# One change to a four-layer transformer kernel: the second attention's scores issued by number, a third stack buffer, updates behind the stacks, function tables loaded ahead

## The chip, the cores and the metric

The kernel runs on one core of a Trainium2 chip. A core has TensorE (PE, matrix products; its weight loads are listed as PEld), VectorE (DVE), ScalarE (ACT), GpSimd (POOL) and SyncE (SP, which issues DMAs). Each engine works through its own queue in order, and the queues meet only through semaphores. The metric is the device time of one execution in microseconds (us), lower is better.

## The reference

Tokens are 2 sequences (b) of 512 positions with 256 features, in 8 tiles of 128 tokens. Four layers run one after the other, each of the same form:

```python
for l in range(4):
    xn = layernorm(x)
    s = attn[l](xn)
    g = silu(ffn[l](xn))
    x = x + s * g
```

Layer 0: causal attention of 16 heads of 16, then a mixture of 8 experts with a shared one, sigmoid gated. Layer 1, the one the change is about, has 16 query heads, 4 key heads and no mask:

```python
q, k = rms_norm(xn @ Wq), rms_norm(xn @ Wk); v = xn @ Wv
q, k = rope(q), rope(k)
probs = softmax(einsum('btkgh,bskh->bkgts', q * H**-0.5, k))
out = einsum('bkgts,bskh->btkgh', probs, v) @ Wo
```

Its FFN sends every token to 2 of 8 experts. Layers 2 and 3 are causal attentions of 16 heads of 128 with plain FFNs of 1024 hidden features (GELU), the last one with ternary weights and a 4-bit rounding of its output.

## The kernel before

All work is written out by hand, one block per engine; the order within an engine is the order of the calls in its block, and nothing reorders it. Waits count: `x.wait_ge(sem, n)`.

**Stacks.** Scores of layers 0 and 1 are kept exact with bf16 matrices: every query and key of 16 numbers is split into three bf16 parts and stacked into 96 rows. In layer 1 a tile m (8 of them, 4 per sequence) takes this path: PE projects it (`project1`, line 761), ACT takes it out of the bank with its squares (`take`), POOL and DVE rotate it, ACT writes the first parts (`stack1_first`, lines 1412 to 1414), DVE the remainders (`stack1_rest`, 1901), POOL the middle parts (`stack1_middle`, 520), DVE the last ones (`stack1_last`, 1911), PE transposes the stack (`stack1_transpose`, 728: 20 matrices into three banks), and ACT and DVE copy it out (`stack1_copy`, 1366, and `stack1_copies`, 1920 to 1924). Tiles 0 to 3 do so while layer 0's FFN ends (`ffn0`), tiles 4 to 7 inside the loop of the second attention. The last four have two buffers (`STK1B`), so tile 6 waits for tile 4's transposes and tile 7 for tile 5's.

**Second attention.** `attention1` has 32 steps s, four to a unit u (a sequence and a group of 4 heads). In step s ACT takes 4 exponentials (line 1482) of 128x512 scores out of banks 0, 1, 2 in turn into one of two halves of PT. PE computes scores n = 4s to 4s+3 (line 882), each into bank n % 3, so score n waits for exponential n-3. `values(s)` (line 893) multiplies the 4 probabilities of step s with V into bank 4 and waits for all four. The order on PE is

```python
scores(0)
for s in range(UNITS1 * TPB):
    if s + 1 < UNITS1 * TPB: scores(s + 1)
    if s % TPB == 0 and s > 0: turn_outputs(s // TPB - 1)
    values(s)
    ...   # s 3: layer norm transposes; 4, 5, 6: project1; 10-13: stack transposes; 15: ranks
```

At a unit's end DVE stores bank 4 (`store_outputs`, 1984), PE turns it (`turn_outputs`, 901) and DVE divides (`normalise`, 1974 and 1975); the first `values` of a unit waits for the store of the unit before. ACT has its own extra work behind the exponentials of a step: two copies after step 4, `take` after 5 (two), 6 and 7, `router_act` after 8, `stack1_first` after 9 to 12. DVE works through rotations, the router's small operations (`probabilities`, `largest`, `chosen`, `slots`, some 0.25 us each) and stacks in an order written out.

**End of the first FFN.** `ffn0` computes 13 hidden chunks per sequence: PE (line 1159) into one of three pairs of banks, ACT a sigmoid (1629), POOL or DVE (600, 2169) the weighting, DVE the product (`hidden`, 2170 and 2174), and PE's chunk after the next two waits for that product. Four tiles of output follow per sequence: `down` on PE (1177), `tail` on DVE (2159), `post` on ACT (1635), `update` on DVE (2153 to 2155, into X). `post` and `update` have two pairs of buffers. For the second sequence they are mixed with the stacks of tiles 0 to 3.

**Function tables.** ACT holds one set of functions. Where the next activation needs another, the program has an ACT_TABLE_LOAD right ahead of it; copies need none.

## Time and profile before

| | us |
|---|---|
| median of 3 runs (lowest, highest) | 1364.73 (1360.65, 1364.87) |
| the profiled execution's own time | 1354.29 |
| span of its trace | 1352.5 |
| PE busy | 1223.2 (90%) |
| DVE, ACT, POOL busy | 731.8, 604.8, 122.9 |
| mean granted TensorE clock, share of full | 0.984 |

The profile's page has the busy time of each engine, the span in 40 slices, and the chain that ended last: from the last instruction back, at each step to what released it. The timeline lists instructions in order of time: start in us from the span's start, duration, engine, line, operation, written tile <- read tile with their shapes, how many equal ones were merged, and in brackets how long the engine stood idle before them and who released it. The view by windows gives busy time per engine (with the number of instructions), the granted clock as a share of 2.4 GHz, the share of DMA time, and GB/s. Instructions overlap in their pipelines: four exponentials of 0.6 us start 0.49 us apart.

### The profile page before, as it was taken

What the parts mean: (1) busy time and instruction counts of PE and PEld (TensorE: products, weight loads), DVE (VectorE), ACT (ScalarE), POOL (GpSimd) and SP (SyncE); (2) the same over time, 40 slices, a digit from 0 to 9 for tenths busy, and PEclk for the clock granted to TensorE, in tenths of its full rate; (3) what the DMA queues carried; (4) which work ended last, traced back from release to release, by engine and by line L of the source; (5) the groups of instructions that cost most, each with busy time, mean ns of one, the idle gap of its engine ahead of it and who ended that gap; (6) DMA issues with size and microseconds to landing.
All of it is one profiled execution on the core that took longest, in us unless ns stands there. A gap on an engine that the chain in (4) does not pass through costs nothing.

```text
span 1352.5 us, 18754 instructions
## 1 busy us (share of the span) xinstructions
PE 1223.2 (90%) x6390; PEld 763.2 (56%) x6396; DVE 731.8 (54%) x2031; ACT 604.8 (45%) x1511; POOL 122.9 (9%) x144
## 2 busy tenths in 40 slices
PE   5988878878899979999999899999999999999994
PEld 4634444423276545656565587656666666667853
DVE  3776627826143478787878720444444444447257
ACT  2634543677822224545455402444454454442053
POOL 3320013421400400000000000000000000000000
PEclk9989999999999989999999999999999999999998
DMA  8001000320222400000000002100000000000000
GB/s 245 1 18 41 33 27 0 103 72 1 94 78 90 187 12 12 12 12 13 8 8 8 1 0 74 67 24 12 24 12 24 13 24 16 20 12 1 1 0 31
DMA packets 28046, 48.66 MB, mean 36 GB/s; under 512 B 3902, under 2 KB 22302, under 8 KB 26886
## 3 DMA queue, kind: packets, MB, share of 16 engines
q1 hardware_dynamic: 25222, 38.13, 8.8%
q0 software_dynamic: 2736, 9.37, 2.4%
q8 instruction: 53, 0.87, 0.3%
q14 instruction: 35, 0.29, 0.1%
HBM read 40.36 MB, written 9.19 MB: 37 GB/s over the span
## 4 chain that ended last, share of the span: by engine, by line
PE 67%; DVE 13%; issue 11%; ACT 6%; POOL 2%; DMA 1%; SPq 0%; ACTq 0%; POOLq 0%; DVEq 0%
PE bank L975 13%; PE bank L991 9%; PE bank L982 8%; PE bank L968 5%; PE bank L960 5%; PE bank L986 4%; PE bank L893 2%; PE bank L1221 2%; PE bank L882 2%; PE bank L1312 2%; PE bank L1239 2%; PE bank L1159 2%; PE bank L814 1%; ACT PT L1482 1%; PE bank L1299 1%
## 5 line engine op out<-in xcount | busy, mean ns | idle before, releaser
L1366 ACT COPY R<-bank 128x512 f32<-128x512 f32 (+4 forms) x199 | 106.3, 551 | 319.9 <-PE bank L991 142.8
L2052 DVE CUSTOM_DVE_ANT_0 bank<-bank,mask_row 128x128 f32<-128x128 f32 (+3 forms) x256 | 127.1, 497 | 173.2 <-PE bank L982 170.8
L975 PE MATMUL bank<-XNT,W 128*128 128x512 f32 x416 | 200.2, 605 | 7.4 <-ACT R L1366 3.8
L1511 ACT ACTIVATE R<-bank,nm 128x128 f32<-128x128 f32 (+3 forms) x256 | 136.2, 532 | 109.0 <-DVE nm L2052 108.1
L982 PE MATMUL bank<-R 128*128 128x512 f32 (+3 forms) x384 | 134.3, 434 | 0.0
L975 PEld LDWEIGHTS bank<-XNT,W 128*128 128x128 f32 x416 | 75.1, 191 | 100.9 <-issue 92.3
L960 PE MATMUL bank<-W,R 128*128 128x256 f32 x576 | 125.3, 380 | 3.2 <-ACT R L1366 3.2
L960 PEld LDWEIGHTS bank<-W,R 128*128 128x128 f32 x576 | 109.1, 190 | 18.7 <-ACT R L1366 2.1
L986 PE MATMUL bank<-identf,R 128*128 128x128 f32 x640 | 112.4, 275 | 7.1 <-DVE R L2069 5.5
L991 PE MATMUL bank<-PT,R 128*128 128x128 f32 (+3 forms) x384 | 112.0, 435 | 5.6 <-ACT PT L1366 4.3
L1366 ACT COPY PT<-bank 128x128 f32<-128x128 f32 (+3 forms) x256 | 108.6, 426 | 15.2 <-PE bank L986 15.1
L986 PEld LDWEIGHTS bank<-identf,R 128*128 128x128 f32 x640 | 79.2, 141 | 59.1 <-issue 33.7
L991 PEld LDWEIGHTS bank<-PT,R 128*128 128x128 f32 x384 | 71.2, 190 | 61.4 <-issue 37.8
L968 PEld LDWEIGHTS bank<-W,XNT 128*128 128x128 f32 x640 | 76.5, 192 | 9.5 <-issue 7.6
L968 PE MATMUL bank<-W,XNT 128*128 128x128 f32 x640 | 77.9, 275 | 0.0
L1482 ACT ACTIVATE PT<-bank 128x512 f32<-128x512 f32 x128 | 66.0, 607 | 15.1 <-PE bank L882 15.1
L1956 DVE TENSOR_REDUCE W<-bank 128x1 f32<-128x128 f32 (+3 forms) x128 | 55.9, 485 | 25.2 <-PE bank L778 24.9
L1471 ACT ACTIVATE PT<-bank 128x512 f32<-128x512 f32 (+3 forms) x128 | 46.2, 438 | 37.9 <-PE bank L804 37.5
L982 PEld LDWEIGHTS bank<-R 128*128 128x128 f32 x384 | 58.2, 191 | 1.1 <-issue 0.5
L882 PE MATMUL bank<-R 96*128 96x512 bf16 x128 | 40.9, 404 | 18.8 <-ACT PT L1482 17.8
L2069 DVE TENSOR_SCALAR R<-R,erec 128x128 f32<-128x128 f32 (+3 forms) x128 | 50.4, 394 | 5.2
L2115 DVE TENSOR_SCALAR R<-R,erec 128x128 f32<-128x128 f32 (+3 forms) x128 | 49.5, 387 | 5.1
(282 smaller groups left out, 1811.9 us busy)
## 6 DMA issues: line engine op xcount, KB each, us to landing
W<-in_wq SPq DMA_DIRECT2D x32, 128.0 KB, 2.0
W<-in_wo SPq DMA_DIRECT2D x2, 2048.0 KB, 11.4
W<-in_egu SPq DMA_DIRECT2D x1, 2816.0 KB
W<-in_wk SPq DMA_DIRECT2D x20, 128.0 KB, 2.1
W<-in_wv SPq DMA_DIRECT2D x20, 128.0 KB, 2.0
R<-xg SPq DMA_DIRECT2D x5, 512.0 KB, 4.7
yg<-R SPq DMA_DIRECT2D x5, 512.0 KB, 3.1
W<-in_wa SPq DMA_DIRECT2D x2, 1024.0 KB, 5.0
```

The source lines that it names most:

```text
L882: ins = mm(PS[n % 3][:, :], kstk[0:KQ, g, b * SEQ + j * P:b * SEQ + (j + 1) * P], qstk[0:KQ, g * GH + h, b * SEQ:(b + 1) * SEQ], start=Tru ...
L960: ins = mm(PS[4 + m % 4][:, 0:D], heads[:, k, m * P:(m + 1) * P], w[:, k, :], start=k == 0, stop=k == n - 1)
L968: ins = mm(bank[:, t * P:(t + 1) * P], XNT[:, c, b * SEQ + t * P:b * SEQ + (t + 1) * P], wqkv23[:, 2, c, :], start=c == 0, stop=c == DC - 1)
L975: ins = mm(bank[:, :], wqkv23[:, s, c, :], XNT[:, c, b * SEQ:(b + 1) * SEQ], start=c == 0, stop=c == DC - 1)
L982: return mm(PS[u % 4][:, 0:n], q[:, t * P:n], k[:, 0:n], start=True, stop=True)
L986: ins = tr(PS[4 + u % 2][:, j * P:(j + 1) * P], Pr[u % 4][:, j * P:(j + 1) * P], identf[:, :])
L991: ins = mm(PS[6][:, j * P:SEQ], v[:, j, :], PT[:, slot, j, j * P:SEQ], start=j == 0, stop=j == TPB - 1)
L1366: return nc.scalar.copy(dst, src)
L1482: fn(PT[:, s % 2, h, :], PS[n % 3][:, :], ACT.Exp, scale=HD ** -0.5).then_inc(cb["pb_ready"], 1)
L1511: return fn(Pr[c][:, 0:n], PS[c][:, 0:n], ACT.Exp, scale=-1.0, bias=nm[:, c:c + 1], accum_out=esum[:, c:c + 1])
L1956: dve.tensor_reduce(nmx[b][:, t, h:h + 1], PS[banks[i % len(banks)]][:, 0:(t + 1) * P], AX.X, ALU.max, negate=True).then_inc(smax_used, 1)
L2052: return dve.tensor_tensor_reduce(out=s[:, 0:n], in0=s[:, 0:n], in1=mask_row[:, SEQ - n:SEQ], scale=-1.0, scalar=-MASKED, op0=ALU.add, op1 ...
```

## The change

Seven edits, none of which changes a number that is computed:

1. `scores` in `attention1` counts single matrices instead of steps. Step s issues scores up to 4s+6, then `values(s)`, then scores up to 4s+9, and only then `turn_outputs` and the step's extra work. The waits of every score are as before.
2. Extra work is regrouped: `project1(7)` with `project1(6)` in step 5, both `take` after step 6, `stack1_first` one step earlier (8 to 11), `router_act` behind the second of them.
3. `STK1B` has three buffers, so that only tile 7 waits for a transpose (tile 4's). `RES1B` moves to R1.
4. On DVE, `probabilities(1)` and `largest(0)` go between and behind the first stacks of the loop.
5. `update` of tile 3 goes behind `hidden(1, 3)`, the updates of tiles 4 to 7 behind the last stack's copies. For that, tiles 4 to 7 have buffers of their own.
6. ACT's order at the end of `ffn0` is new.
7. A one-column activation `preload(func)` makes ACT load a table early: Sigmoid after the first attention, Exp ahead of the last stack's copy, Silu after the second attention, Exp after two FFNs, Gelu after attentions 2 and 3, Silu after the last hidden chunk.

```diff
-        STK1B = [R2[:, 2048 + 960 * i:3008 + 960 * i].bitcast(BF16).rearrange("p (h k e) -> p h k e", k=BLK, e=HD)
-                 for i in range(2)]
+        STK1B = [R2[:, 1024 + 960 * i:1984 + 960 * i].bitcast(BF16).rearrange("p (h k e) -> p h k e", k=BLK, e=HD)
+                 for i in range(3)]
...
-            return (STK1[m % 3], RES1[m % 2]) if m < TPB else (STK1B[m % 2], RES1B[m % 2])
+            return (STK1[m % 3], RES1[m % 2]) if m < TPB else (STK1B[m % 3], RES1B[m % 2])
...
+                issued = [0]
+
+                def scores(upto):
+                    for n in range(issued[0], min(upto + 1, UNITS1 * TPB * GH)):
+                        s, h = n // GH, n % GH
...
+                        if n % (NG * TPB * GH) == 0:
+                            pe.wait_ge(stk_act, 2 * NT + TPB)
+                            pe.wait_ge(stk_dve, 2 * NT + STACKS_A + STACKS_B * b)
                         pe.wait_ge(cb["pb_ready"], n + 1 + GH - 3)
...
+                    issued[0] = max(issued[0], upto + 1)
...
-                scores(0)
                 for s in range(UNITS1 * TPB):
-                    if s + 1 < UNITS1 * TPB:
-                        scores(s + 1)
+                    scores(s * GH + 6)
+                    values(s)
+                    scores(s * GH + 9)
                     if s % TPB == 0 and s > 0:
                         turn_outputs(s // TPB - 1)
-                    values(s)
...
                         project1(6)
-                    elif s == 6:
                         project1(7)
...
+            def preload(func):
+                fn(small[:, 62:63], mhalf[:, 0:1], func)
...
-                elif m >= TPB + 2:
-                    act.wait_ge(stk_ps, 4 * NT + 3 * (m - 1))
+                elif m == TPB + 3:
+                    act.wait_ge(stk_ps, 4 * NT + 3 * (TPB + 1))
...
                         take(6)
-                    elif s == 7:
                         take(7)
-                    elif s == 8:
-                        router_act(1)
-                    elif s in (9, 10, 11, 12):
-                        stack1_first(s - 5)
+                    elif s in (8, 9, 10, 11):
+                        stack1_first(s - 4)
+                        if s == 9:
+                            router_act(1)
...
                 stack1_first(1)
-                post(4)
-                post(5)
                 stack1_first(2)
                 stack1_copy(0)
-                post(6)
+                post(4)
                 stack1_first(3)
                 stack1_copy(1)
+                post(5)
+                post(6)
+                stack1_copy(2)
                 post(7)
-                stack1_copy(2)
+                preload(ACT.Exp)
                 stack1_copy(3)
...
                     if t >= 1:
                         update(t - 1)
-                    if t == TPB - 1:
-                        update(t)
                     hidden(1, t)
+                update(TPB - 1)
...
                 stack1_copies(3)
-                update(7)
+                for tile in range(TPB, NT):
+                    update(tile)
```

The other `preload` calls and the regrouped lines on DVE are as the list says.

PE in the second attention from the values of step 27 to those of step 29 before (line 882 scores, 893 values, 901 the turn of a unit's outputs):

```order
L893 MATMUL bank4<-PT,R2 32x512 x4
L882 MATMUL bank2<-R1 128x512
L882 MATMUL bank0<-R1 128x512
L882 MATMUL bank1<-R1 128x512
L882 MATMUL bank2<-R1 128x512
L901 MATMUL bank6<-identf,R2 128x128 x4
L893 MATMUL bank4<-PT,R2 32x512 x4
L882 MATMUL bank0<-R1 128x512
L882 MATMUL bank1<-R1 128x512
L882 MATMUL bank2<-R1 128x512
L882 MATMUL bank0<-R1 128x512
L893 MATMUL bank4<-PT,R2 32x512 x4
```

and of the changed kernel, the same stretch (886 scores, 897 values, 905 the turn):

```order
L897 MATMUL bank4<-PT,R2 32x512 x4
L886 MATMUL bank1<-R1 128x512
L886 MATMUL bank2<-R1 128x512
L886 MATMUL bank0<-R1 128x512
L886 MATMUL bank1<-R1 128x512
L897 MATMUL bank4<-PT,R2 32x512 x4
L886 MATMUL bank2<-R1 128x512
L886 MATMUL bank0<-R1 128x512
L886 MATMUL bank1<-R1 128x512
L905 MATMUL bank6<-identf,R2 128x128 x4
L886 MATMUL bank2<-R1 128x512
L897 MATMUL bank4<-PT,R2 32x512 x4
```

The third score of a step's successors stays ahead of the values, the fourth and two more come behind them, and the turn stands behind those instead of ahead of the values.

ACT at the end of `ffn0` before (1412 to 1414 `stack1_first`, 1366 a stack's copy, 1635 `post`, 1482 the first exponentials):

```order
L1366 COPY R1<-bank0 96x8x128
L1635 ACTIVATE R2<-R2 128x256
L1412 ACTIVATE PT<-R1,small 128x16x48
L1413 ACTIVATE PT<-R1,small 128x8x16
L1414 ACTIVATE PT<-R1,small 128x4x16
L1366 COPY R1<-bank3 96x8x128
L1635 ACTIVATE R2<-R2 128x256
L1366 COPY R1<-bank0 96x8x128
L1366 COPY R1<-bank3 96x8x128
L1482 ACT_TABLE_LOAD
L1482 ACTIVATE PT<-bank0 128x512
```

and of the changed kernel (1417 to 1419, 1368, 1639; 1371 is `preload`; the first exponential is the next row):

```order
L1368 COPY R1<-bank0 96x8x128
L1639 ACTIVATE R2<-R2 128x256
L1417 ACTIVATE PT<-R1,small 128x16x48
L1418 ACTIVATE PT<-R1,small 128x8x16
L1419 ACTIVATE PT<-R1,small 128x4x16
L1368 COPY R1<-bank3 96x8x128
L1639 ACTIVATE R2<-R2 128x256 x2
L1368 COPY R1<-bank0 96x8x128
L1639 ACTIVATE R2<-R2 128x256
L1371 ACT_TABLE_LOAD
L1371 ACTIVATE small<-mhalf 128x1
L1368 COPY R1<-bank3 96x8x128
```

Both `post` calls of tiles 5 and 6 are behind the last `stack1_first`, and the table load has moved from ahead of the exponentials to ahead of the last stack's copy.

DVE at the end of the first sequence's outputs before (2159 `tail`, 2153 to 2155 `update`, 2170 `hidden`, 1766 statistics):

```order
L2159 TENSOR_TENSOR R2<-bank7,XN 128x256
L2153 TENSOR_TENSOR R2<-R2 128x256
L2154 TENSOR_TENSOR R2<-R2 128x256
L2155 TENSOR_TENSOR X<-X,R2 128x256
L2153 TENSOR_TENSOR R2<-R2 128x256
L2154 TENSOR_TENSOR R2<-R2 128x256
L2155 TENSOR_TENSOR X<-X,R2 128x256
L2170 TENSOR_TENSOR W1<-R1,bank4 128x512
L1766 BN_STATS stat<-X 128x6 x4
```

and of the changed kernel (2171, 2165 to 2167, 2182, 1778):

```order
L2171 TENSOR_TENSOR R2<-bank7,XN 128x256
L2165 TENSOR_TENSOR R2<-R2 128x256
L2166 TENSOR_TENSOR R2<-R2 128x256
L2167 TENSOR_TENSOR X<-X,R2 128x256
L2182 TENSOR_TENSOR W1<-R1,bank4 128x512
L2165 TENSOR_TENSOR R2<-R2 128x256
L2166 TENSOR_TENSOR R2<-R2 128x256
L2167 TENSOR_TENSOR X<-X,R2 128x256
L1778 BN_STATS stat<-X 128x6 x4
```

The second `update` (tile 3) now stands behind the product that PE waits for.

## Rows read from the trace of the kernel before

**Rows 1.** The page's chain that ended last, shares of the span by engine.

```profile
PE 67%; DVE 13%; issue 11%; ACT 6%; POOL 2%; DMA 1%; SPq 0%; ACTq 0%; POOLq 0%; DVEq 0%
```

**Rows 2.** Timeline, a plain step and a turn step: start, us, engine, line, op.

```profile
340.03 2.06 ACT L1482 ACTIVATE PT<-bank 128x512 f32<-128x512 f32 x4 [0.39 <-PE bank L882]
340.68 0.39 PE L882 MATMUL bank<-R 96*128 96x512 bf16 x1 [0.32 <-ACT PT L1482]
341.00 1.07 PE L893 MATMUL bank<-PT,R 128*32 128x512 f32 x8
342.00 0.82 PE L882 MATMUL bank<-R 96*128 96x512 bf16 x3
342.49 2.06 ACT L1482 ACTIVATE PT<-bank 128x512 f32<-128x512 f32 x4 [0.39 <-PE bank L882]
...
343.36 0.60 PE L901 MATMUL bank<-identf,R 128*128 128x128 f32 x4
...
345.38 0.60 ACT L1482 ACTIVATE PT<-bank 128x512 f32<-128x512 f32 x1 [0.83 <-PE bank L882]
```

**Rows 3.** Timeline of ACT, attention's first exponentials, two waits, last exponentials.

```profile
268.09 4.03 ACT L1482 ACTIVATE PT<-bank 128x512 f32<-128x512 f32 x8
...
301.74 0.26 ACT L1378 ACTIVATE rt<-rt 128x64 f32<-128x64 f32 x1 [2.08 <-DVE rt L1800]
...
317.40 0.94 ACT L1412 ACTIVATE R<-R,small 128x768 bf16<-128x768 f32 x1 [1.35 <-PE bank L728]
...
368.37 2.07 ACT L1482 ACTIVATE PT<-bank 128x512 f32<-128x512 f32 x4 [0.39 <-PE bank L882]
```

**Rows 4.** Timeline of PE: last stack's transposes, first scores, one projection.

```profile
263.91 1.29 PE L728 MATMUL bank<-identb,PT 128*96 128x128 bf16 x20 [3.11 <-DVE PT L1913]
266.13 1.44 PE L882 MATMUL bank<-R 96*128 96x512 bf16 x3 [0.93 <-ACT R L1366]
...
290.34 1.59 PE L761 MATMUL bank<-W,XNT 128*128 128x393 f32 x4
```

**Rows 5.** Timeline of DVE: the last stack's remainders.

```profile
260.74 0.48 DVE L1901 SCALAR_TENSOR_TENSOR PT<-R,small,PT 128x256 f32<-128x256 f32 x1 [0.45 <-ACT PT L1414]
```

**Rows 6.** Timeline of ACT: the function table ahead of the first exponential.

```profile
266.80 1.28 ACT L1482 ACT_TABLE_LOAD   x1 [1.23 <-PE bank L882]
```

**Rows 7.** Timeline of all engines, first FFN: its start and its half's end.

```profile
191.05 2.54 PE L1159 MATMUL bank<-R,W 128*128 128x512 bf16 x11
191.43 1.28 ACT L1629 ACT_TABLE_LOAD   x1
...
226.09 2.54 POOL L600 TENSOR_TENSOR R<-R,W 128x512 f32<-128x512 f32 x2 [4.98 <-ACT R L1629]
...
226.24 1.38 DVE L2153 TENSOR_TENSOR R<-R 128x256 f32<-128x256 f32 x1
...
230.02 3.67 PE L1159 MATMUL bank<-XNT,W 128*88 128x512 f32 x8 [3.56 <-DVE W L2170]
...
233.50 1.38 DVE L1776 TENSOR_SCALAR XN<-X,mv,rstd 128x256 f32<-128x256 f32 x4
```

**Rows 8.** Timeline, start of the fourth layer's FFN.

```profile
1288.14 2.54 PE L1325 MATMUL bank<-R,W 128*128 x11 [0.42 <-ACTq L1716]
1288.14 1.28 ACT L1721 ACT_TABLE_LOAD   x1
```

**Rows 9.** Timeline of DVE: eighth stack's copies, then output store of unit 3.

```profile
325.95 0.69 DVE L1920 COPY R<-bank 96x1024 bf16<-96x1024 bf16 x1 [1.52 <-PE bank L728]
...
331.52 0.69 DVE L1984 COPY R<-bank 128x512 f32<-128x512 f32 x1 [0.34 <-PE bank L893]
```

**Rows 10.** Timeline of SP: the first loads of sorted rows for the experts.

```profile
362.01 15.70 SPq L424 DMA_DIRECT2D R<-xg  x3
```

**Rows 11.** Windows: PE, PEld, DVE, ACT, POOL busy us; granted clock; DMA share; GB/s.

```profile
266.00:273.00 7.00, 5.69 (x17) 1.05 (x18) 4.38 (x16) 5.31 (x9) 1.27 (x2) 0.52 0.99 269
...
329.30:370.50 41.20, 36.04 (x225) 9.54 (x223) 10.15 (x36) 33.09 (x65) 16.58 (x19) 1.00 0.22 77
```

55 lines of the change are left out of this document (27 added, 28 removed).

## The prediction, made before the changed kernel ran

> **What bounds the kernel now.** I read the page's chain first: two thirds of the span are matrix work of PE [rows 1], most of it in layers 2 and 3, which the change leaves alone but for some table loads. What it touches lies between 191 and 371 us, so there I read the timeline, and in it who ended each wait.
>
> In the second attention, the steps from 16 on show the rhythm [rows 2]. Call the end of a step's last exponential E. PE issues a score 0.05 after the exponential that frees its bank (340.03 + 0.60 is 340.63; the score starts at 340.68), `values` 0.32 later, the next score 1.00 after that (342.00), its exponential 0.49 later, and 0.61 later that has ended: 0.05 + 0.32 + 1.00 + 0.49 + 0.60 = 2.46 us, and the steps are 2.46 apart. ACT alone would need 4 x 0.49 = 1.96. So it is a ring of both engines, with each idle for part of it. A step with `turn_outputs` takes 345.38 - 342.49 = 2.89: the turn stands inside the ring and adds 0.43. All 32 steps take 370.44 - 268.09 = 102.35 us [rows 3]. Of these 4.03 are the first two steps [rows 3] and 30 x 2.46 = 73.8 the rhythm of the rest; 24.5 us are excess, from turns and from the extra work of steps 3 to 15.
>
> Ahead of it, PE stands 3.11 us for the last stack of tile 3, then 0.93 for ACT's last copy [rows 4], and ACT loads the Exp table for 1.28 when the first scores are already there [rows 6].
>
> **Part one: start of the first FFN.** The Sigmoid load ends at 192.71. PE's first chunk is four of the eleven matmuls that take 2.54 from 191.05 [rows 7], so ready at about 192.1. The load moves ahead of ACT's copies, where ACT waits for PE. Gain 0.6 at most, and the ring of chunk, sigmoid, weighting and product carries it on; if DVE's or POOL's start is bound otherwise, 0. I take 0.5.
>
> **Part two: `update(3)` behind `hidden(1, 3)`.** Before, DVE does the update from 226.24 while POOL works on two weightings in a row (2.54 for both), its first operation lasts 1.38, and PE stands 3.56 until 230.02 [rows 7]. The product needs POOL's first weighting, 226.09 + 1.27 = 227.4, plus 0.7 on DVE: PE can go on at 228.1, 1.9 sooner. But the update now falls under POOL's second weighting, statistics and normalisation still start when they did, and the layer norm's transposes wait for the scaling, 233.50 to 234.9 [rows 7]. PE's next two chunks wait for products that DVE has no sooner. What is left of the 1.9 at those transposes is 0.8. Bounds 0.2 and 1.9; I take 0.8.
>
> **Part three: the stacks of tiles 0 to 3.** Tile 2's transposes end at 263.91 - 3.11 = 260.80. Tile 3's wait because DVE has updates and `tail` between its pieces and its remainder waits 0.45 for ACT [rows 5], which did `post` calls first. In the new order ACT's first parts of tile 3 come at about 254.8, DVE's remainder at 258.2 (behind the copies of tile 1), POOL's parts by 260.0, DVE's last part by 260.5: tile 3's transposes follow tile 2's without a wait and end at 262.1. DVE's copies end near 263.0. ACT: copy of tile 2 until 261.0, `post(7)` 0.35, table load 1.28 [rows 6], the one-column activation 0.2, copy of tile 3 with 1.0: 263.8. So the load now holds up the last copy. Scores follow as before, 0.55 behind the copy, at 264.35, and the first exponential about 0.6 later at 264.9, against 268.09 [rows 3]: 3.2 us. Lower bound 1.3 (only the load leaves the scores), upper bound 3.11 + 1.28 = 4.4. The four updates, some 1.4 each, now run beside the first exponentials until 268.5; with statistics (1.8), POOL's 1.4 and the scaling (1.4) the second half's normalised tiles are ready at 273. The transposes that read them come at about 277, so this is covered by 4 us; without cover it would cost what is missing one for one.
>
> Here the Trainium skill speaks against the change: "ScalarE: Activation LUTs", section "What ACT_TABLE_LOAD costs", puts a switch at 1283 ns of load and about 1380 ns of drain, 2.66 us in total. The load here is 1.28, and the activation starts as it ends, at 268.09 with no second gap [rows 3, 6]. By the page the last copy would be held 1.38 longer than I have it and the sum would be 9.3 instead of 10.7.
>
> **Part four: scores by number.** Put the ring together again. Score 4s+6 needs exponential 4s+3, `values(s)` needs the same one, then come 4s+7 to 4s+9. From E: 0.05 + 0.32 + 1.00 + 0.49 + 0.60, again 2.46. The order doesn't shorten a plain step; it only cuts the ring at another exponential. But PE has issued score 4s+9 at E + 2.0 and needs to be back only at E + 2.5, so a turn (0.43) fits there. Seven turns gain 7 x 0.43 = 3.0, and `ranks` (0.4) goes the same way, as far as the store of unit 3 lets it.
>
> For steps 3 to 15 I followed both queues with the durations of the rows: exponentials 0.49 apart, a score 0.21, `values` 1.0, a projection 1.43 [rows 4], its `take` 0.98, `stack1_first` 1.37 [rows 3], a stack's transposes 1.25 (1.29 with the last one's drain) [rows 4], DVE's copies of a stack 1.54 [rows 9]. Counted from the first exponential, step 1 ends at 5.48 (later than before, since `values(0)` now stands ahead of its last score) and then 30 steps of 2.46 give 79.3. To this come as excess: step 5 0.8 (layer norm copies), 6 3.8 and 7 3.3 (four projections and their takes, little better than before), 9 to 11 2.8 (`stack1_first`, with the exponentials stalled behind it), 12 2.1 (tile 7's buffer waits for tile 4's transposes), 13 and 14 1.9, 15 2.0 (tile 7's transposes wait 1.4 for DVE's copies of tile 6), 17 0.4 (the store of unit 3 is behind `largest` and `chosen`; before, these and the copies filled DVE from 325.95 to 331.52 [rows 9]). That is 17.2 in place of 24.5, and the whole 96.5 against 102.35: 5.8 us, turns included. Gone are the 2.08 that ACT waits for the router [rows 3], since first stack work now stands ahead of it, and part of the waits of 1.35 for a stack's transposes [rows 3]. Lower bound 3.0, the turns alone; upper bound 10, if DVE's waits vanish too.
>
> **The clock.** From 266 to 273 the granted clock is 0.52 of full, that is the 1.2 GHz level, after PE had stood for 3.11 and 0.93 us; from 329.3 to 370.5 it is 1.00 [rows 4, 11]. But it had stood 3.56 us before 230.02 [rows 7], and the matmuls behind that ran at full speed (3.67 for 8). With one wait of 2.3 instead of two, full speed at the first scores would gain 0.9 more (`values(0)` 1.7 against 1.0, and a score); I take 0.4 between 0 and 0.9.
>
> **Part five: the other loads.** Each is worth 1.28 at most. The one ahead of the last FFN starts at 1288.14 together with PE's matmuls, of which the first chunk is six of eleven in 2.54, so 1.4: it was hidden [rows 8]. The others stand where ACT waits for PE anyway. The eight one-column activations are 0.2 each, one of them counted above. I take 0 for all; bounds -0.5 and 1.3.
>
> **What comes behind.** The experts need rows that POOL scatters; the first load is issued at 362.01 [rows 10], 8.4 us before the last exponential ends, and it depends on `normalise(5)`, which moves with the loop. It stays covered by some 4 us.
>
> **Sum.** 0.5 + 0.8 + 3.2 + 5.8 + 0.4 = 10.7 us. The profiled execution took 1354.29, so 1343.6 in its terms; its span of 1352.5 becomes 1341.8. The median of the runs is 10.4 higher; I carry the difference over to it: 1364.73 - 10.7 = 1354.0.
>
> **The rivals.** *The load hurts more where it stands now*: the last stack's copy is held by more than the 1.28, say by as much again, and 1.4 are lost: 1355.4. Against it: no gap behind a load [rows 3, 6]. 0.09. The drain in "ScalarE: Activation LUTs" of the Trainium skill (section "What ACT_TABLE_LOAD costs") would do just this; so far the trace does not bear it out. *A new wait takes the old one's place*: DVE's queue, with its many small operations, is late with a store or a copy in steps 10 to 17, and in the stack part only the load's 1.3 is won: 0.5 + 0.8 + 1.3 + 3.0 = 5.6, 1359.1. For it: my working of 13 steps has a dozen meeting points, and any error there costs. 0.18. *The scores' order does nothing*: a plain step keeps 2.46 in any case, and if the turn's bank isn't stored in time, it falls back into the ring; then 2.6 is left, 1362.1, no measurable change. Against it: the store starts right behind `values` and takes 0.7, while the turn stands 1.6 behind the next step's start. 0.12. *Slower*: the clock. The new order spreads PE's waits differently, and if PE is granted 1.2 GHz in the loop, a plain step grows by about 0.7 for `values`, 0.2 for the third score and 0.2 for the next: 1.1. It takes back the gain after 10 steps and is slower by over 0.3% from the 14th; 31 steps give 1364.7 - 10.7 + 34 = 1388. Against it: 1.00 in the same loop before, with as much waiting [rows 2, 11]. 0.05.
>
> **How the numbers follow.** A measurement of this kernel can tell 0.3%, about 4 us. My forecast of 1354.0 has 0.56. Faster: 0.56 + 0.09 + 0.18 = 0.83; within 0.3%: 0.12; slower: 0.05. The parts' bounds around the forecast and the new wait's 1359 give 1347 to 1361; the runs' own spread of 4 us is inside that.
>
> **What would show it.** Step distances of 2.46 at the turns (wrong: 2.9). The first exponential about 4.5 sooner (0.5 + 0.8 + 3.2), near 263.6. The table load directly ahead of the last stack's copy, and no wait for tile 3's transposes. The last exponential near 360.2. PE back at about 228 in the first FFN, but only 0.8 ahead at the layer norm's transposes. It would be wrong if PE stands for DVE in steps 10 to 17 longer than 2 us in all, or if the granted clock falls below 1.00 in the loop.

## The result, and the profile after

| | before | after |
|---|---|---|
| median of 4 runs (lowest, highest), us | 1362.86 (1360.65, 1364.87) | 1348.22 (1345.48, 1350.60) |
| ratio, 95% interval | | 0.9896 (0.9878 to 0.9915) |
| the profiled execution's own time, us | 1354.29 | 1347.06 |
| span of its trace, us | 1352.5 | 1345.3 |
| mean granted clock | 0.984 | 0.984 |

The change gains 14.2 us by the ratio, where 10.7 were forecast; the two traces differ by only 7.2. Both gaps need an account, and most of the experiments went into it. In the table above, before has four runs. The forecast was counted down from the 1364.73 of three of them, so 1.9 us of the distance between 1354.0 and 1348.22 lies in that starting point.

The page of after has its first lines and its chain as follows; the chain is as in [rows 1], since what the change touches is a tenth of the span.

```profile
span 1345.3 us, 18762 instructions
PE 1225.4 (91%) x6396; PEld 765.1 (57%) x6396; DVE 731.3 (54%) x2031; ACT 605.4 (45%) x1518; POOL 121.5 (9%) x144
PE 69%; DVE 13%; issue 10%; ACT 7%; POOL 1%; DMA 0%; SPq 0%; ACTq 0%; POOLq 0%; DVEq 0%
```

**Start of the first FFN** (timeline of after, PE and ACT). The Sigmoid load is gone from ahead of the first sigmoid, which starts 1.06 behind PE's chunk. PE's two chunks with a wait start 11.22 us (185.40 to 196.62) behind the out projection, against 12.05 (183.83 to 195.88) before: 0.8 gained. The out projection itself started 1.57 later than in the first trace of before, where nothing is changed.

```profile
192.41 2.75 PE L1161 MATMUL bank<-R,W 128*128 128x512 bf16 x12
193.47 0.60 ACT L1633 ACTIVATE R<-bank 128x512 f32<-128x512 f32 x1 [0.49 <-PE bank L1161]
196.62 3.03 PE L1161 MATMUL bank<-R,W 128*128 128x512 bf16 x12 [1.46 <-DVE R L2182]
```

**Update of tile 3 behind the product** (timeline of after, the rows that answer to [rows 7]). PE's wait is 1.65 instead of 3.56. But the normalisation (DVE L1788) now lasts 2.22 instead of 1.38, beside POOL's weighting of 234.61, and the second pair of transposes waits for it. The first project starts at 237.78.

```profile
228.84 3.67 PE L1161 MATMUL bank<-XNT,W 128*88 128x512 f32 x8 [1.65 <-DVE W L2182]
234.04 2.22 DVE L1788 TENSOR_SCALAR XN<-X,mv,rstd 128x256 f32<-128x256 f32 x4
234.61 1.18 POOL L602 TENSOR_TENSOR R<-R,W 128x512 f32<-128x512 f32 x1 [0.93 <-ACT R L1633]
236.31 0.66 PE L683 MATMUL bank<-identf,XN 128*128 128x128 f32 x4 [0.66 <-DVE XN L1788]
237.78 5.68 PE L763 MATMUL bank<-W,XNT 128*128 128x393 f32 x16
```

**Stacks of tiles 0 to 3** (timeline of after, answering to [rows 3, 4, 6]). The transposes of tiles 2 and 3 are one row of 40. The load stands ahead of the last copy and holds it up, the scores follow 0.06 behind the copy, and the granted clock is 1.00 from the first score on, where it was 0.52 [rows 11].

```profile
259.85 2.52 PE L730 MATMUL bank<-identb,PT 128*96 128x128 bf16 x40
261.40 0.42 ACT L1639 ACTIVATE R<-R 128x256 f32<-128x256 f32 x1
261.84 1.28 ACT L1371 ACT_TABLE_LOAD   x1
263.24 0.99 ACT L1368 COPY R<-bank 96x1024 bf16<-96x1024 bf16 x1
264.29 0.82 PE L886 MATMUL bank<-R 96*128 96x512 bf16 x3 [1.91 <-ACT R L1368]
264.77 3.54 ACT L1487 ACTIVATE PT<-bank 128x512 f32<-128x512 f32 x7 [0.54 <-PE bank L886]
```

**The loop** (timeline of after). Answering to [rows 2]: plain steps are 2.40 apart, not 2.46 (332.00, 334.40), and a step with a turn is 2.41 (357.51 to 359.92, the turn at 357.75) instead of 2.89. The loop takes 362.92 - 264.77 = 98.15 against 102.35. Three of its steps are 3.95, 3.52 and 3.65 long, though nothing but scores, values and one turn is in them: 3.9 us together. The rows show two kinds of time in them. In the first and the third, ScalarE stands although its scores are ready. The second is TensorE at half clock behind the first: `values` takes 1.94 instead of 1.06, and the granted clock is 0.54 from 339 to 342. In the kernel without early loads (below) the clock stays at 1.00 behind the same first pause, and the step is 2.42. "Pauses" below means the sum of both kinds.

```profile
332.00 2.06 ACT L1487 ACTIVATE PT<-bank 128x512 f32<-128x512 f32 x4 [0.33 <-PE bank L886]
334.40 2.06 ACT L1487 ACTIVATE PT<-bank 128x512 f32<-128x512 f32 x4 [0.33 <-PE bank L886]
338.35 2.06 ACT L1487 ACTIVATE PT<-bank 128x512 f32<-128x512 f32 x4 [1.89 <-PE bank L886]
341.87 2.06 ACT L1487 ACTIVATE PT<-bank 128x512 f32<-128x512 f32 x4 [1.45 <-issue]
345.52 2.06 ACT L1487 ACTIVATE PT<-bank 128x512 f32<-128x512 f32 x4 [1.58 <-PE bank L886]
357.75 0.60 PE L905 MATMUL bank<-identf,R 128*128 128x128 f32 x4
362.32 0.60 ACT L1487 ACTIVATE PT<-bank 128x512 f32<-128x512 f32 x1 [0.33 <-PE bank L886]
```

PE in the second of these steps, the window of after (columns: stretch, its length, busy time and instructions of PE, PEld, DVE, ACT, POOL, then the granted clock, DMA share, GB/s), and the like window of the kernel without early loads:

```profile
339.36 1.94 PE L897 MATMUL bank<-PT,R 128*32 128x512 f32 x8
339.00:342.00 3.00, 2.99 (x11) 0.58 (x12) 0.00 (x0) 1.55 (x4) 2.13 (x3) 0.54 0.24 87
```

```profile
341.00:344.00 3.00, 2.74 (x17) 0.62 (x20) 0.00 (x0) 2.67 (x6) 2.09 (x4) 1.00 0.24 87
```

### The profile page after: what moved, and what is told of

Its sections match the earlier page's. It is cut to its first block, busy times and chain, and to the rows that moved or that the text cites. A ratio compares the mean times of both kernels' runs of the same rounds, so it can differ in the third digit from the quotient of the medians.

```text
span 1345.3 us, 18762 instructions
## 1 busy us (share of the span) xinstructions
PE 1225.4 (91%) x6396; PEld 765.1 (57%) x6396; DVE 731.3 (54%) x2031; ACT 605.4 (45%) x1518; POOL 121.5 (9%) x144
## 4 chain that ended last, share of the span: by engine, by line
PE 69%; DVE 13%; issue 10%; ACT 7%; POOL 1%; DMA 0%; SPq 0%; ACTq 0%; POOLq 0%; DVEq 0%
PE bank L977 13%; PE bank L993 9%; PE bank L984 8%; PE bank L962 5%; PE bank L970 5%; PE bank L988 4%; PE bank L1223 2%; PE bank L886 2%; PE bank L897 2%; ACT PT L1487 2%; PE bank L1314 2%; PE bank L1274 2%; PE bank L1241 2%; PE bank L816 1%; PE bank L1301 1%
## 5 line engine op out<-in xcount | busy, mean ns | idle before, releaser
L1968 DVE TENSOR_REDUCE W<-bank 128x1 f32<-128x128 f32 (+3 forms) x128 | 56.1, 484 | 26.1 <-PE bank L780 25.8
```

The lines of the kernel that those rows point to most:

```text
L1968: dve.tensor_reduce(nmx[b][:, t, h:h + 1], PS[banks[i % len(banks)]][:, 0:(t + 1) * P], AX.X, ALU.max, negate=True).then_inc(smax_used, 1)
```

## The experiments

**How they are read.** One trace is one draw, so each is cut into stretches that can be set side by side: from the first `down` of the first FFN to the first exponential, the loop, and the units of the loop, counted between DVE's stores (`store_outputs`). A unit without other work is 10.27 us in the old order of scores, 9.60 in the new one, 10.03 with the turn in the ring and some 11.96 with the values in halves; what stands above that in units six and seven is called pauses. All lengths are in us. The changed kernel was also run a second time without an edit ("after, again"). It was expected, before that run, to have pauses of 2.5 to 4.5 us at the same steps if they are the usual case, and a first unit of 10.8 at full clock if the early Exp load is what keeps the clock. Both came: 3.9 and 10.8.

| kernel | ratio to before (95%) | `down` to 1st exp. | loop | first unit | units 2 to 4 | units 6, 7 | pauses |
|---|---|---|---|---|---|---|---|
| before, first trace | | 56.1 | 102.35 | 12.4 | 19.2, 16.4, 15.4 | 10.3, 10.3 | 0 |
| before, again | 0.999 (0.9973 to 1.0007) | 57.6 | 106.5 | 12.3 | 19.2, 16.4, 15.4 | 14.5, 10.3 | 4.2 |
| scores alone | 0.9929 (0.9907 to 0.9950) | 57.0 | 102.7 | 12.7 | 17.3, 13.4, 19.0 | 13.1, 10.0 | 3.9 |
| regrouping alone | 0.9969 (0.9938 to 1.0000) | 57.0 | 105.3 | 13.1 | 18.4, 15.4, 13.2 | 15.6, 11.2 | 6.3 |
| FFN end alone | 0.9957 (0.9941 to 0.9972) | 52.4 | 107.4 | 12.9 | 19.2, 15.7, 15.7 | 15.2, 10.3 | 5.0 |
| after | 0.9896 (0.9878 to 0.9915) | 52.1 | 98.15 | 10.8 | 17.6, 16.2, 13.3 | 12.4, 10.7 | 3.9 |
| after, again | 0.9909 (0.9882 to 0.9937) | 52.1 | 98.2 | 10.8 | 17.6, 16.2, 13.3 | 12.5, 10.7 | 3.9 |
| no early loads | 0.9902 (0.9877 to 0.9927) | 52.4 | 98.6 | 12.4 | 17.6, 16.2, 13.3 | 12.4, 9.5 | 2.7 |
| no early Exp | 0.9914 (0.9894 to 0.9933) | 52.4 | 98.6 | 11.9 | 17.6, 16.2, 13.3 | 12.4, 10.0 | 3.2 |
| update 3 as before | 0.9899 (0.9880 to 0.9919) | 53.9 | 98.2 | 10.8 | 17.6, 16.2, 13.3 | 12.5, 10.7 | 4.0 |
| turn in the ring | 0.9920 (0.9901 to 0.9940) | 52.1 | 101.7 | 10.8 | 17.1, 16.2, 12.3 | 16.4, 10.7 | 7.1 |
| late scatters | 0.9988 (0.9970 to 1.0005) | 52.1 | 106.2 | 11.9 | 17.6, 16.2, 13.3 | 9.6, 9.6 | 11.7, in unit 8 |
| tanh | 0.9876 (0.9847 to 0.9905) | 51.1 | 96.95 | 10.8 | 17.6, 16.2, 13.3 | 12.4, 9.5 | 2.7 |
| values in halves | 0.9968 (0.9954 to 0.9983) | 52.1 | 108.5 | 14.2 | 18.4, 16.2, 14.1 | 12.0, 12.0 | 0 |

### The kernel before, once more

No edit.

> The kernel before, unchanged, once more: it sizes what differs between two executions of one program, since the profiled one of before took 1354.29 us and its timed ones 1360.65 to 1364.87. Theory A, the traced execution was a short draw: ratio 1.000 (within 0.2%), and a second trace has a span some 4 to 10 us above 1352.5, with the surplus in stretches that the change doesn't touch (start of the input loads, layer 0, layers 2 and 3), while the second attention keeps 102.35 us. Theory B, a profiled execution of before is always some 8 us short of its timed ones: span again near 1352. Theory C, the surplus lies in the second attention or the first FFN: then what the change gains is more than the first trace shows.

A span of 1365.5, 13.0 above the first trace. It lies in four places: 1.9 ahead of the first `down`, 1.5 from there to the layer norm's transposes, 4.1 in the loop, 4.5 between the experts and the shared expert, the rest 1.0. Theory A holds for the ratio and for the draw, but not for the place: 5.6 of the 13.0 lie where the change works, so theory C is right there. The first trace of before, on which the prediction was built, happened to have neither the half clock in the first FFN nor the pauses in the loop. The timeline of this trace, PE and ACT, at both places:

```profile
231.86 5.17 PE L1159 MATMUL bank<-XNT,W 128*88 128x512 f32 x8 [3.56 <-DVE W L2170]
...
343.25 2.07 ACT L1482 ACTIVATE PT<-bank 128x512 f32<-128x512 f32 x4 [0.39 <-PE bank L893]
345.71 2.06 ACT L1482 ACTIVATE PT<-bank 128x512 f32<-128x512 f32 x4 [0.39 <-PE bank L893]
350.58 2.06 ACT L1482 ACTIVATE PT<-bank 128x512 f32<-128x512 f32 x4 [2.80 <-remote]
351.77 1.94 PE L893 MATMUL bank<-PT,R 128*32 128x512 f32 x8
354.86 1.08 ACT L1482 ACTIVATE PT<-bank 128x512 f32<-128x512 f32 x2 [2.21 <-PE bank L893]
...
365.57 2.06 ACT L1482 ACTIVATE PT<-bank 128x512 f32<-128x512 f32 x4 [0.39 <-PE bank L893]
```

The same wait of 3.56 as in [rows 7] is followed here by 5.17 us for the 8 matmuls that took 3.67. In the loop the step from 345.71 to 350.58 is 4.87; behind the first pause `values` takes 1.94 instead of 1.06, so it costs clock as well. The last row names `values` (L893) as what an exponential waited for; it is used below.

### Scores by number alone

```diff
-                        scores(s + 1)
+                    scores(s * GH + 6)
+                    values(s)
+                    scores(s * GH + 9)
```

> The kernel before with edit 1 alone (scores by number, values ahead of the last three, turn behind them). The prediction's own terms: turns 3.0, ranks 0.4, a plain step unchanged at 2.46, so the loop takes about 99.0 instead of 102.35 and the ratio is 0.9975. Rival 1, the plain step is shortened too (the trace of after has steps of 2.40): 28 x 0.06 = 1.7 more, loop 97.3, ratio 0.996. If the steps are 2.46 here, the 2.40 belongs to something else. Rival 2, the order does nothing: the turn falls back into the ring, turn steps of 2.89, loop 102, ratio 1.000.

Plain steps are 2.40 apart here too, and turns stand outside them. The loop without its 3.9 of pauses is 98.8, 3.5 less than 102.35: nearer the first forecast (99.0) than rival 1 (97.3), though the shorter step is real, so rival 1 has the mechanism and not the size. The shares differ: units two and three lose 5.0, unit four gains 3.6 (the stacks' extra work now falls into it), and the plain units lose 0.67 each. The time fell by more than that (9.7 by the ratio, 6.8 at the least); this trace is the slowest of its six timed runs, so the loop's 3.5 is what is shown for the edit, and the rest is not accounted for.

### Regrouping alone

```diff
-            return (STK1[m % 3], RES1[m % 2]) if m < TPB else (STK1B[m % 2], RES1B[m % 2])
+            return (STK1[m % 3], RES1[m % 2]) if m < TPB else (STK1B[m % 3], RES1B[m % 2])
```

with the regrouped `project1`, `take`, `stack1_first`, and DVE's order.

> The kernel before with edits 2 to 4 alone (extra work regrouped, third stack buffer, DVE's small operations behind the first stacks), scores in the old order. From the traces without pauses: the whole change takes 8.1 us from the loop, the scores' order alone 3.5, the clock at its start 1.7, so 2.9 should be left for this part: unit lengths of about 18.9, 16.4, 14.0 and 10.3 for the second to fifth instead of 19.24, 16.41, 15.41 and 10.61, loop 99.9 plus the pauses, ratio 0.998. Rival, regrouping works only together with the scores' order (before it, extra work on PE stands ahead of fewer scores): under 1 us, ratio 1.000.

Units two to four are 0.9, 1.0 and 2.2 shorter, the loop without its 6.3 of pauses is 99.0, against the 99.9 expected; the first unit is 0.7 longer. By the trace the rival (works only together) is out: 3.5 and 3.3 for the two parts apart, and 6.4 together once the clock is taken out (below). The time alone can't tell it, since its interval reaches 1.0000.

### The end of the first FFN alone

```diff
+                update(TPB - 1)
...
+                for tile in range(TPB, NT):
+                    update(tile)
```

with ACT's new order and the buffers; no early load.

> The kernel before with edits 5 and 6 alone (updates behind, ACT's new order, own buffers), no table load moved. Theory A: the new order removes PE's 3.11 us before tile 3's transposes, and the Exp load stays on the path wherever it stands: the copy of tile 3 ends near 263, the load follows the first score, the first exponential is about 3.4 sooner than 268.09, near 264.7; ratio 0.9975. The early load is then worth 0.4 or less. Rival, the load ahead of the copy is what brings its full 1.28: the first exponential only 2.0 sooner, near 266, ratio 0.9985. Part two (the update behind the hidden chunk) should show PE back 1.9 sooner near 228 but only 0.2 left at the layer norm's second pair of transposes, through a scaling that takes 2.2 instead of 1.4 beside POOL's weighting.

The first exponential comes 3.8 sooner, counted from `down` and against the first trace of before (5.2 against the second, of which 1.5 are the half clock). Theory A holds, also in that an early load brings little by itself: after gains only 0.3 more up to here. The part on the update came as well: PE waits 1.65, the scaling takes 2.22, and the first project starts 25.09 behind `down`, against 25.20 before.

### Without the early loads

All eight one-column activations are taken out of the changed kernel.

> The changed kernel without the one-column activations, so that every function table is loaded where it is first needed, all else as after. Theory A: the Sigmoid load costs 0.8 again, the Exp load 0.3 (it moves from ahead of the last copy to behind the first score), the six others nothing: 1.1 us, ratio to the changed kernel 1.0008, not to be told from it by time; against before about 0.990. Rival: part of the 14 us that the timed runs show over the 10.7 of the sum comes from the loads ahead of the experts, FFNs 2 and 3 and the attentions behind them, 1.3 each: up to 5 us slower than the changed kernel, 0.993 against before, and the trace shows layers 2 and 3 longer by that.

By time not to be told from the changed kernel, and layers 2 and 3 have the same length within 1 us, so the rival is out. PE's second wait of the FFN's start ends 12.05 behind the out projection again, against 11.22, so the Sigmoid load costs its 0.8 as expected. `down` to the first exponential is 0.3 longer. What I had not expected is the first unit: 12.4 instead of 10.8.

### Without the early Exp load

```diff
-                preload(ACT.Exp)
                 stack1_copy(3)
```

> The changed kernel without the one early Exp load ahead of the last stack's copy, all other edits and loads as in it. Theory A: the load's place itself is worth only 0.3 us (without it the load follows the first score, and the last copy ends 1.3 sooner), but it joins PE's two waits (0.9 and 1.6 us in the trace without any early load) into one of 1.9, after which the clock is granted in full; so here the granted clock falls to half from about 265 to 271 and the first unit takes 12.4 instead of 10.8: together 2.0 us, 0.0015 of the time. Rival: the half clock in that trace came from elsewhere (it is a draw, or comes from the Sigmoid load): first unit 10.8, clock 1.00, and at most 0.3 us lost.

The windows of after and then of this kernel (columns: stretch, its length, busy time and instructions of PE, PEld, DVE, ACT, POOL, then the granted clock, DMA share, GB/s):

```profile
265.00:268.00 3.00, 2.38 (x13) 0.54 (x12) 2.83 (x8) 3.00 (x7) 0.00 (x0) 1.00 1.07 456
268.00:271.00 3.00, 2.74 (x18) 0.67 (x15) 2.00 (x9) 2.37 (x5) 0.76 (x2) 1.00 0.93 214
```

```profile
265.00:268.00 3.00, 2.70 (x12) 0.55 (x12) 2.83 (x8) 2.85 (x6) 0.00 (x0) 0.77 0.95 398
268.00:271.00 3.00, 3.00 (x16) 0.54 (x12) 1.42 (x8) 1.66 (x4) 1.27 (x2) 0.66 1.03 232
```

and the timeline of this kernel, PE and ACT:

```profile
262.56 0.81 PE L886 MATMUL bank<-R 96*128 96x512 bf16 x3 [0.93 <-ACT R L1368]
263.02 1.28 ACT L1487 ACT_TABLE_LOAD   x1 [1.01 <-PE bank L886]
264.97 1.93 PE L886 MATMUL bank<-R 96*128 96x512 bf16 x4 [1.59 <-ACT PT L1487]
266.83 1.94 PE L897 MATMUL bank<-PT,R 128*32 128x512 f32 x8
```

Theory A, with 1.4 instead of 2.0 us. The load behind the first score makes PE stand twice, 0.93 and 1.59, around three matmuls; then a part of the first steps runs at half clock, `values` at 1.94. With the load ahead of the copy PE stands once, 1.91. Over all traces: without an early Exp load all seven ran at half clock here; with it five of seven stayed at full speed (first unit 10.8; one of them, the tanh below, waits only 0.93), while those of the late scatters and of the values in halves fell to it behind the same wait of 1.91. So the load's place is worth 0.3 by itself, and 1.2 to 1.7 of clock in most executions, not in all. The time (0.9914 against 0.9896 and 0.9909) can't tell this, and with so few traces the link between the shape of the waits and the clock is likely, but not proved.

### The update of tile 3 back in its place

```diff
                         update(t - 1)
+                    if t == TPB - 1:
+                        update(t)
                     hidden(1, t)
```

> The changed kernel with the update of tile 3 back ahead of the hidden chunk's product. It sizes part two of the prediction (0.8, bounds 0.2 and 1.9). Theory A: PE stands 3.5 instead of 1.7 at the fourth chunk, but the normalisation is then clear of GpSimd's weighting and takes 1.38 instead of 2.22, so only 0.2 us are lost at the first project of tile 0; ratio as the changed kernel's, and the first exponential 0.2 later counted from the out projection. Theory B, the scaling's 2.22 has another cause and stays: then 0.8 to 1.0 are lost.

```profile
230.87 5.36 PE L1161 MATMUL bank<-XNT,W 128*88 128x512 f32 x8 [3.58 <-DVE W L2182]
234.36 1.38 DVE L1788 TENSOR_SCALAR XN<-X,mv,rstd 128x256 f32<-128x256 f32 x4
239.71 5.73 PE L763 MATMUL bank<-W,XNT 128*128 128x393 f32 x16
```

The mechanism of theory A is there: the scaling is back at 1.38. The Trainium skill, "SBUF — State Buffer", section "Terms", says that DVE and GpSimd take a shared port in turn and the loser blocks; 2.22 beside POOL's weighting and 1.38 without agree with it. But the loss is 1.9 and not 0.2 (first exponential 53.9 behind `down` instead of 52.1), and neither theory had it: behind a wait of 3.58 the chunk takes 5.36 instead of 3.67, half clock, as in the second trace of before. This long wait is in five traces; the chunk behind it ran slow in two and at full speed in three. Behind the short wait of 1.65 it ran at full speed in all nine traces that have it. Without the half clock (1.7) the loss is the 0.2 of theory A. The timed runs (0.9899) don't show the loss.

### The turn in the ring again

```diff
+                    if s % TPB == 0 and s > 0:
+                        turn_outputs(s // TPB - 1)
                     values(s)
                     scores(s * GH + 9)
-                    if s % TPB == 0 and s > 0:
-                        turn_outputs(s // TPB - 1)
```

> The changed kernel with the turn ahead of the step's values, as before the change, and the scores still by number. Theory A (the prediction's part four): the turn comes back into the ring at 0.43 a time, 6 times in the loop outside the long steps: units five to seven 10.0 instead of 9.6, loop 2.6 to 3.0 us longer, ratio to before 0.992. Rival 1, the plain step's 2.40 instead of 2.46 comes with the turn's place: then units are 10.27 as before the change. Rival 2, the turn waits for the store of the last unit and now holds the values up: 1.2 a time, 7 us longer.

A turn costs 0.43 to 0.53 where a unit has nothing else (fifth 9.66 against 9.13, eighth 9.70 against 9.27), as theory A has it, and plain steps stay 2.40, so rival 1 is out. But units two and four are 0.4 and 1.0 shorter: without its pauses the loop is 94.6 against 94.2. The seven turns, 3.0 in my sum, are worth about 0.4 net. So theory A's 2.6 to 3.0 for the loop is wrong, though its price of one turn is right. What makes this kernel's loop 3.5 longer are its pauses, 7.1 against 3.9.

### The scatters moved

```diff
-        SCATTER_AT = {5: (0, 1, 2), 6: (3, 4, 5), 7: (6, 7)}
+        SCATTER_AT = {7: (0, 1, 2, 3, 4, 5, 6, 7)}
```

> The changed kernel with all 16 scatters of GpSimd in its last unit (from about 350 us) instead of 6, 6 and 4 in the last three (from 328 us); nothing is left out. It takes away what I suspect behind the pauses of ACT in the loop. Theory A, the scatters' transfers hold up something that ACT needs (its next instructions, or the landing of its semaphores): no step above 2.45 between 325 and 349 us, unit six 9.6 instead of 12.4, and pauses, if any, behind 352; the experts start some 6 us later since the last scatter is issued at about 370 instead of 355. Theory B, ACT's own refill of instructions makes the pauses and the scatters have no part in it: they stand at the same steps as before, 2.8 to 3.9 us. Total about 5 us slower than the changed kernel by the late rows under A, 8 under B.

Timeline of this kernel, ACT, and POOL's first scatter:

```profile
336.95 2.06 ACT L1487 ACTIVATE PT<-bank 128x512 f32<-128x512 f32 x4 [0.33 <-PE bank L886]
339.34 2.06 ACT L1487 ACTIVATE PT<-bank 128x512 f32<-128x512 f32 x4 [0.33 <-PE bank L886]
341.74 2.06 ACT L1487 ACTIVATE PT<-bank 128x512 f32<-128x512 f32 x4 [0.33 <-PE bank L886]
344.17 1.17 POOL L561 DMA_INDIRECT xg<-XN,rt  x1 [0.48 <-issue]
352.72 1.58 ACT L1487 ACTIVATE PT<-bank 128x512 f32<-128x512 f32 x3 [1.72 <-PE bank L886]
361.23 1.57 ACT L1487 ACTIVATE PT<-bank 128x512 f32<-128x512 f32 x3 [5.07 <-remote]
```

Units six and seven are 9.6 and 9.6, to the hundredth free of pauses, and the eighth, with all 16 scatters in a row, has 11.7 us of them. The pauses go where the scatters go, and no other trace has any in its eighth unit. In all twelve traces with pauses, ScalarE's first idle time over 1 us that follows the first scatter starts 6.8 to 9.6 us behind it (328.33 and 336.46 in after, 340.49 and 347.78 in the second of before, 344.17 and 351.00 here). So the scatters' place sets the pauses' place, by one trace of this edit and the timing in the others. Scatters alone are not enough: two traces have them and no pause. By what path they act is open. The engines' own refill of instructions, which the profile lists as a DMA queue of its own ("instruction"), is not it by itself: such packets lie in the stretch of 333 to 334 here and in that of 344 to 345 in the first trace of before, and no pause follows either. In time this kernel is 10.9 us slower than the changed one on the same chip (1358.98 against 1348.09), and not 5 as theory A had it: its pauses are 7.8 longer, and the last exponential to the shared expert's last product takes 100.5 instead of 96.5.

### The last sigmoid as a tanh

```diff
+                    if tile == NT - 1:
+                        fn(gpost0[tile], fpost0[tile], ACT.Tanh, scale=0.5).then_inc(f["g"], 1)
...
                 post(6)
+                preload(ACT.Exp)
                 stack1_copy(2)
-                post(7)
-                preload(ACT.Exp)
                 stack1_copy(3)
+                post(7)
...
+                        own(stt(g, g, 1.0, fpost0[tile], ALU.add, ALU.mult))
+                        own(stt(g, g, 0.5, S[:, tile, :], ALU.mult, ALU.mult))
```

> The changed kernel with its last sigmoid of the first FFN written as a tanh (0.5 tanh(x/2) + 0.5, the same number of DVE operations), which the table of the exponentials also holds: the Exp table is then loaded in ACT's idle time of 1.56 us ahead of the third copy, and the last copy goes first. Theory A, the load holds up the last stack's copy: that copy starts at about 262.0 instead of 263.24, the first exponential comes 1.0 to 1.2 us sooner, and the clock stays at 1.00 since PE waits only 0.9 instead of 1.9; 1.1 us in all, ratio to before 0.001 below that of the changed kernel. Rival, DVE's last copy (ends at 263.2) sets the scores: only 0.2 are gained. Rival 2, tanh forces a table load of its own between the exponentials: 1.3 to 2.6 slower.

```profile
255.37 1.28 ACT L1371 ACT_TABLE_LOAD   x1
256.91 1.01 ACT L1368 COPY R<-bank 96x1024 bf16<-96x1024 bf16 x1
258.16 1.01 ACT L1368 COPY R<-bank 96x1024 bf16<-96x1024 bf16 x1 [0.24 <-PE bank L730]
259.07 0.41 ACT L1640 ACTIVATE R<-R 128x256 f32<-128x256 f32 x1
260.20 3.53 ACT L1487 ACTIVATE PT<-bank 128x512 f32<-128x512 f32 x7 [0.71 <-PE bank L886]
```

The load fills ACT's idle time, the last copy starts 1.5 sooner, and the first exponential comes 1.0 sooner; the tanh needs no load. This is the fastest kernel of the study: 1343.69 us against 1348.09 of the changed one on the same chip. The trace accounts for 1.0 of the 4.4 by the edit and 1.2 by smaller pauses, which differ from trace to trace; the rest is open, and the intervals of the two ratios overlap.

### Values in halves

`values(s, half)` issues two heads, after the exponentials of these two.

```diff
-                    scores(s * GH + 6)
-                    values(s)
-                    scores(s * GH + 9)
+                    scores(s * GH + 4)
+                    if s % TPB > 0:
+                        values(s, 0)
+                    scores(s * GH + 6)
...
+                    values(s, 1)
+                    scores(s * GH + (9 if s in (3, 4, 5, 10, 11, 12, 13, 15) else 7))
```

> The changed kernel with the values of a step split in two: heads 0 and 1 after the second exponential of the step, heads 2 and 3 after the fourth, with scores 4s+5 and 4s+6 between them; PE no longer needs all four exponentials for all of its values. Theory A, the step of 2.40 is a ring (0.05 + 0.39 + 1.0 + 0.43 + 0.60), and not the load of an engine: ACT needs 1.96 and PE some 2.05 a step, so a plain step falls to about 2.1, and with some 20 such steps the loop is 5 to 6 us shorter, near 92; ratio to before 0.985. Rival, two heads alone take nearly as long as four (1.06 for four, which overlap in the array): PE becomes the bound at 4 x 0.22 + 2 x 0.8 = 2.5, and the loop is 2 us longer. Rival 2, the scores behind the second half come too late and the step stays 2.40.

```profile
353.65 1.05 PE L897 MATMUL bank<-PT,R 128*32 128x512 f32 x4
354.64 0.60 PE L886 MATMUL bank<-R 96*128 96x512 bf16 x2
355.18 1.05 PE L897 MATMUL bank<-PT,R 128*32 128x512 f32 x4
```

4 matmuls of two heads take 1.05 us, 8 of four heads take 1.06 (after, 334 to 363 us). The first rival, and sharper than put: splitting doubles PE's time for values, most steps are 3.04, and the loop is 10.4 longer, or 14.3 without after's pauses. The Trainium skill, "TensorEngine Tiling (Array Packing)", section "Key Properties", says that different tiles of the array can execute their matmuls in parallel. The rows agree: four heads on four column tiles take no longer than two heads on two. This version has no pauses although the scatters are there, and is the only one besides the first trace of before.

## Why the prediction was right, and where its sum was short

The forecast of 1354.0 stood for 10.7 us; 14.2 came, 1348.22, near the lower end of the range. The mechanism was right in its outline, but that the total comes near is in part luck: within part four the turns brought some 3 us less than reckoned and the rest 3.6 more, and the trace that it was built on was a fast draw. Point by point, against the first trace of before:

- **Part one**, 0.5: measured 0.8. The ring handed on more of the load's 1.28 than I took.
- **Part two**, 0.8: without the clock 0.1 (`down` to the first project 25.20 before, 25.08 after), below the lower bound of 0.2. The step that failed is that the product and scaling behind the update would keep their durations: the scaling grew from 1.38 to 2.22 beside POOL. With the long wait gone, no half clock followed it in nine traces; it cost 1.5 and 1.7 in the two where it struck, and the sum had it at nothing. I had read [rows 7], full speed behind a wait of 3.56, as the rule; it was one draw.
- **Part three**, 3.2: 3.9 by after's trace and 3.6 without the early load. The load ahead of the copy holds it up as worked out (the copy ends at 264.23; forecast 263.8, and after's trace is later by 1.57 - 0.8 - 0.1, some 0.6, at that point), but scores follow the copy by 0.06 and not 0.55 [rows 6]. The load in that place is worth 0.3 of it.
- **The clock** at the first scores, 0.4, bounds 0 and 0.9: measured 1.2 to 1.7 where it comes, above its bound; the term is mis-sized. The bound was priced from one `values` and one score; the whole first unit is shorter, by 1.2 in the kernel without the Exp load and 1.7 in that without any.
- **Part four**, 5.8: the loop without pauses went from 102.35 to 98.15 - 3.9 = 94.2, so 8.1, of which some 1.7 is the clock; 6.4 are left. The total is close, the split is not. Turns, 3.0 in the sum, are 0.4 net. A plain step is 2.40 and not 2.46, which I had said the order can't do. The failed step is the ring itself: I closed it over the score behind `values`, 0.49 before its exponential [rows 2]. In the old order that exponential is the first of a step and also waits for `values` to be done with its half of PT; the second trace of before names L893 as its releaser in 3 of the 11 steps with this wait, while the first trace names the score every time. In the new order it is a step's last one, needs the score alone, and follows by 0.43. Over some 28 steps that is 1.7. The 0.06 itself is seen in all traces of the two orders; that the wait for PT is its cause is read from the order and the releasers, and no run tests it alone. Of the two waits I read there, the 2.08 for the router is gone as forecast, and one for a stack's transposes is still 1.20.
- **Part five**, 0: right within 1 us.
- **What comes behind**: the first expert starts 2.42 behind the last exponential in both traces.

Term by term that is 0.8 + 0.1 + 3.9 + 6.4 + 1.7 = 12.9, against 10.7 forecast. The traces show only 7.2 of it since after's has 1.6 more ahead of 183 us, where nothing was changed, and 3.9 of pauses that the first trace of before lacks (7.2 + 1.6 + 3.9 = 12.7).

**The signs.** Step distances at turns (2.41), the load's place, the missing wait for tile 3 and, less the 1.6 us ahead of 183 us, PE's return and the first exponential (264.77 - 1.6 = 263.2, forecast 263.6) came as said; the 0.8 at the layer norm's transposes didn't. The last exponential ends at 362.92, 2.7 behind the forecast's 360.2, and without the 1.6 and the 3.9 of pauses it would be 2.8 ahead of it. PE stands for DVE in steps 10 to 17 for 1.25 in all, under the 2 us. One sign of being wrong did come: the granted clock falls to 0.54 in the loop, from 339 to 342, behind the first pause. It costs 1.1 us and not the 34 of the slower rival, since it ends with the next step; the working had no term for it.

**The carry-over.** I took the 10.4 between the median of before and its traced execution over to after as one thing that stays. The second trace of before shows what it is: pauses (4.2), a half clock (1.5), 4.5 in the experts, 1.9 ahead of the first `down`. Some of these the change reaches: the half clock is gone, and pauses are 2.7 to 4.0 with the new order of scores (7.1 with the turn in the ring) and 4.2 to 6.3 with the old one, where they occur. These are single traces, so the difference is likely and not shown. The 4.5 in the experts is one idle time of DVE before its third product of the shared expert, with gathers and weight loads under way. In the two traces of before it is 0.37 and 5.03, in the two of after 2.92 and none; the changed kernel and most of its variants have 1 to 4 us less in that stretch than the old ones, the first trace of before excepted. Why is open; no run tests it.

**The rivals.** A load that hurts more didn't come: it starts 0.02 behind the last activation and the next one follows at once. The 1380 ns of drain in the Trainium skill ("ScalarE: Activation LUTs", section "What ACT_TABLE_LOAD costs") shows at none of the places looked at. A new wait in DVE's queue didn't come either: the updates of tiles 4 to 7, statistics and scaling are done at 273.0 and the transposes start at 276.06, a cover of 3.1 where I had counted 4. Scores' order does nothing: out, by plain steps and the loop of the kernel with that edit alone. The slower rival looked at the right quantity. At the loop's start the clock went the other way: with PE's waits drawn together into one it stayed at full speed in five of seven traces, and with two waits around a little work in none. Inside the loop it did fall, for about one step.

## What to carry to other kernels

Where TensorE stands twice around a few matmuls, price the half clock behind it (1.2 to 1.7 us here) and not only the waits, and set one trace's full speed behind a long wait down as a draw until a second trace says so. Ask of each exponential or copy in a ring what else it waits for besides the matmul, such as a buffer half: a reordering that puts another instruction at that point shortens the ring. And before a difference between traced and timed runs is carried over as a constant, find which stretches make it, since the change may reach them.

## What the runs showed of the hardware

- With indirect DMAs of GpSimd under way, one each 1.27 us, ScalarE stands for 1.2 to 5.1 us at a time, from 6.8 to 9.6 us behind the first of them on, in twelve of fourteen traces, though its exponentials use no buffer of theirs. Moved in one kernel, they took the pauses along. The path is open.
- The same wait of 3.56 to 3.58 us of TensorE is followed by 3.67 us for 8 matmuls in three traces, and by 5.17 and 5.36 in two. Behind a wait of 1.65 it was 3.67 in all nine. Two waits of 0.93 and 1.6 around three matmuls were followed by half clock in all three traces that have them, one of 1.91 in two of six.
- Behind such a pause the next `values` took 1.94 us instead of 1.06 at a granted clock of 0.54 (after); without early loads it took 1.06 at 1.00 behind the same pause.
- Four column tiles of 32 in 128x512 fp32 matmuls take 1.06 us together and two of them 1.05.
